# Routed rows written to fixed places per expert, four groups at a time; gathers and sums moved within covariance steps

## What is computed

```python
x = x + _L0_attn_a_ref(_layernorm(x, axis=-1), ...)      # 16 heads of 8, rotary
x = x + _L0_ffn_ref(_layernorm(x, axis=-1), ...)         # attention, then mixture of experts
x = x + _L0_attn_b_ref(_layernorm(x, axis=-1), ...)      # 16 heads of 8, covariance scores
x = x + _L0_ffn_ref(_layernorm(x, axis=-1), ...)
...
def moe_ff(x, w_gate, w1, b1, w2, b2):                   # 8 experts, 128 -> 512 -> 128
    probs = jax.nn.softmax(t @ w_gate, axis=-1)
    tw, ti = lax.top_k(probs, TOP_K)                     # TOP_K = 2
    tw = tw / jnp.sum(tw, axis=-1, keepdims=True)
    for e in range(N_EXPERTS):
        we = jnp.sum(jnp.where(ti == e, tw, 0.0), axis=-1)
        h = jax.nn.gelu(t @ w1[e] + b1[e]) @ w2[e] + b2[e]
        out = out + we[:, None] * h
```

## Time and profile before

| | us |
|---|---|
| median of 3 runs | 901.24 |
| the runs | 893.77, 901.24, 902.31 |
| the profiled execution's own time | 898.2 |
| its span, first to last instruction | 896.4 |
| busy in it: PE / DVE / ACT / POOL | 767.0 / 544.5 / 543.4 / 484.2 |
| mean granted TensorE clock | 0.923 of full speed |

### The profile page before, as it was taken

How to read it: one execution, slowest core, us unless ns; L and a number is a source line. 1 busy time by engine, 2 the same in 40 slices (tenths; PEclk the granted TensorE clock), 3 DMA queues, 4 the chain that set the end, 5 groups by cost and what they waited for, 6 DMA issues and landing times.

```text
span 896.4 us, 21301 instructions
## 1 busy us (share of the span) xinstructions
PE 767.0 (86%) x7166; PEld 546.7 (61%) x7166; DVE 544.5 (61%) x1370; ACT 543.4 (61%) x1264; POOL 484.2 (54%) x906
## 2 busy tenths in 40 slices
PE   1999999999999399697988999999999948968970
PEld 1756655666565189497964565566666525958970
DVE  4699899788988123012486887878889822211232
ACT  0377777878787256154546676787877834715640
POOL 6667678747762621504645665844777273060436
PEclk9999999999999789698999899999999977978995
DMA  9300000000000436266210000000000042635842
GB/s 274 111 3 3 3 2 3 4 3 3 4 2 4 130 107 175 79 182 175 79 38 13 16 18 5 4 3 3 3 3 3 3 124 77 173 103 143 245 124 67
DMA packets 57657, 56.29 MB, mean 63 GB/s; under 512 B 6856, under 2 KB 42448, under 8 KB 57552
## 3 DMA queue, kind: packets, MB, share of 16 engines
q1 hardware_dynamic: 39200, 39.13, 15.5%
q0 software_dynamic: 4096, 8.40, 3.2%
q10 hardware_dynamic: 14256, 7.41, 2.9%
HBM read 40.10 MB, written 14.29 MB: 61 GB/s over the span
## 4 chain that ended last, share of the span: by engine, by line
PE 56%; DVE 21%; issue 11%; POOL 7%; DMA 3%; ACT 2%; another core or an unknown queue 0%; ACTq 0%; POOLq 0%; DVEq 0%; SPq 0%
DVE M L1109 11%; PE bankO L466 11%; PE bankR L720 8%; PE bankE L707 7%; PE bankE L485 7%; PE bankE L439 6%; DVE QKV L1071 2%; POOL Yg L1578 2%; PE bankR L452 2%; PE bankE L476 2%; PE bankR L506 2%; PE bankR L536 1%; PE bankR L738 1%; PE bankR L554 1%; DMA Yg<-sorted_y,SLOT 1%
## 5 line engine op out<-in xcount | busy, mean ns | idle before, releaser
L1109 DVE TENSOR_REDUCE M<-bankR 128x2 f32<-128x512 f32 x512 | 326.4, 684 | 62.7 <-PE bankR L452 56.9
L834 ACT ACTIVATE Pr<-bankE 128x512 f32<-128x512 f32 x512 | 277.7, 595 | 129.5 <-PE bankE L439 109.1
L466 PE MATMUL bankO<-Pr,Vx 128*32 128x256 f32 x2048 | 170.5, 406 | 18.8 <-issue 16.1
L452 PE MATMUL bankR<-KQ 32*128 32x256 f32 x1024 | 171.3, 339 | 5.0 <-DVE M L1109 2.9
L439 PEld LDWEIGHTS bankE<-KQ 32*128 32x128 f32 x1024 | 79.6, 188 | 97.1 <-issue 64.2
L439 PE MATMUL bankE<-KQ 32*128 32x256 f32 x1024 | 133.3, 335 | 0.5 <-issue 0.5
L1312 DVE COPY Yb<-bankR 128x128 f32<-128x128 f32 x92 | 26.4, 290 | 167.9 <-PE bankR L720 111.1
L452 PEld LDWEIGHTS bankR<-KQ 32*128 32x128 f32 x1024 | 110.1, 191 | 17.1 <-DVE M L1109 12.8
L951 ACT ACTIVATE G<-bankE,W 128x128 f32<-128x128 f32 x368 | 101.5, 384 | 24.8 <-PE bankE L707 14.0
L707 PE MATMUL bankE<-XTT,W 128*128 128x128 f32 x736 | 105.1, 288 | 11.4 <-issue 4.6
L1578 POOL DMA_INDIRECT Yg<-sorted_y,SLOT x64 | 62.2, 971 | 95.6 <-DMA sorted_y<-Yb 42.0
(11 more groups left out here) (169 smaller groups left out, 1147.0 us busy)
## 6 DMA issues: line engine op xcount, KB each, us to landing
W<-in_w1b SPq DMA_DIRECT2D x92, 258.0 KB
sorted_y<-Yb ACTq DMA_DIRECT2D x92, 64.0 KB
XT<-sorted_u SPq DMA_DIRECT2D x20, 256.0 KB
sorted_u<-Yg SPq DMA_DIRECT2D x2, 1472.0 KB, 9.7
KQ<-MT SPq DMA_DIRECT2D x128, 4.0 KB
X<-in_x SPq DMA_DIRECT2D x8, 128.0 KB, 7.3
sorted_u<-U,SLOT POOLq DMA_INDIRECT x64
Yg<-sorted_y,SLOT POOLq DMA_INDIRECT x64
```

The source lines that it names most:

```text
L452: k = mm(dve_bank("raw", layer, b, h)[:, z * T:z * T + T], QT[rows, kb, g, z * P:z * P + P], KT[rows, kb, g, :], start=True, stop=True)
L466: k = mm(bankO[SL * j:SL * j + SL, cols], Vx[:, b % VB, kc, HG * g + j, :], Pr[:, g % 2, j, kc, :], start=(g % 2 == 0 and kc == 0), stop=( ...
L834: nc.scalar.activation(Pr[:, (h // HG) % 2, h % HG], act_bank("S", layer, b, h).rearrange("p (k q) -> p k q", k=TT), ACT.Exp, scale=EXP_SC ...
L1109: v.tensor_reduce(M[:, b % 2, :, h], dve_bank("raw", layer, b, h).rearrange("p (t k) -> p t k", t=TT), AX.X, ALU.max, negate=True).then_in ...
```

## The change

The rows of U no longer wait for the totals of a half. `sorted_u` has 1024 places (CAP) for each of the 8 experts, so a row's place needs only the counts of the groups before it. Totals and ranks are made for each block of 8 groups (`do_totals`, `do_rank`, `place_rows`), and `scatter` writes four groups at a time: at the end of steps 16 and 17, twice in step 18 (the second four after 14 of the step's scores), and four times in the mixture, the second four after tile 5 and the last after tile 14. Since a tile of an expert now begins at a row that only the totals tell, `sort_tiles` makes, beside EID, the list ROW of 23 first rows, and `load_x` reads its row from it and loads one tile at a time: 92 transfers of 64 KB, each with a register load, in place of 24. The sorted results stay compact, so a second list, SLOT_Y, is made for the gathers by `place_outputs`. The clearing grows to 8 MB, in eight transfers of 1 MB that ScalarE's queue issues at the head of steps 4 to 11, from G, which GpSimd sets to zero in step 2. `weigh` of block 1 and 3 moves ahead within its step. In the covariance steps the four gathers stand together behind `close`, ahead of `stack_k`, and `combine` goes ahead of `do_max` 4. The gathers of sequences 0 and 1 stand together as well, ahead of the normalisation of sequence 0.

```diff
+BG = GROUPS // 2
+CAP = HB * T
...
-        sorted_u = [nc.dram_tensor(f"sorted_u{k}", (NTL * P, D), F32).ap() for k in range(2)]
+        sorted_u = [nc.dram_tensor(f"sorted_u{k}", (E * CAP, D), F32).ap() for k in range(2)]
...
-            def load_x(ph, q):
-
-                half, i = divmod(GROUP[q][0], NTL)
-                n, k = GROUP[q][1], (ph * NGRP + q) % NXG
+            def load_x(ph, at):
+
+                half, i = divmod(at, NTL)
+                q, j = group_of(at)
+                k = (ph * NGRP + q) % NXG
+                r = sp.value_load(ROW[0:1, half, i:i + 1], min_val=0, max_val=E * CAP - P)
                 if i == 0:
                     sp.wait_ge(scattered[half], 16 * GROUPS * (ph + 1))
-                need(sp, x_turned, ph, q - NXG)
-                sp.dma_start(XT[:, k, 0:n, :],
-                             sorted_u[half][i * P:(i + n) * P, :].rearrange("(j p) d -> p j d", p=P)).then_inc(x_in[k], 16)
+                if j == 0:
+                    need(sp, x_turned, ph, q - NXG)
+                sp.dma_start(XT[:, k, j, :], sorted_u[half][bass.ds(r, P), :]).then_inc(x_in[k], 16)
...
-                for q in range(2 * NXG):
-                    load_x(ph, q)
+                for i in range(2 * NXG * XG):
+                    load_x(ph, i)
                 for at in range(NAT):
                     if at + NW < NAT:
                         load_w(ph, at + NW)
-                    if group_at(at - 1) is not None and group_at(at - 1) % (NGRP // 2) < NGRP // 2 - NXG:
-                        load_x(ph, group_at(at - 1) + NXG)
-                    if at == NTL - XG - 1:
-                        for q in range(NGRP // 2, NGRP // 2 + 2 * NXG):
-                            load_x(ph, q)
+                    if 2 * NXG * XG <= at + 11 < NTL:
+                        load_x(ph, at + 11)
+                    if NTL - XG <= at < NTL + XG:
+                        for i in range(2):
+                            load_x(ph, NTL + 2 * (at - NTL + XG) + i)
+                    if NTL + XG <= at < NAT - 3 * XG:
+                        load_x(ph, at + 3 * XG)
...
+            def do_rank(ph, j):
+
+
+                need(pe, placed, ph, j, 1)
+                ring_r.take(pe, ("rank", ph, j))
+                bank, n = dve_bank("rank", ph, j), BG * E
+                known = slice(0, n * (j % 2 + 1))
+                if j % 2:
+                    mm(bank[:, n:n + E], totals[:], of_expert, start=True, stop=True)
+                mm(bank[:, 0:n], below, OH[:, j * BT:j * BT + BT].rearrange("p n k e -> p (n k e)"), start=True, stop=False)
+                mm(bank[:, 0:n], totals[known, :], earlier_groups[known, of_block(j)], start=False,
+                   stop=True).then_inc(ranked.sem, 1)
+                if j % 2:
+                    ring_r.give(("rank", ph, j), sorted_, ph, j // 2, 1)
...
+            def zero(half, x):
+
+                act.wait_ge(zero_set, 1)
+                act.dma_start(sorted_u[half].rearrange("(p i) d -> p (i d)", p=P)[:, x * ZN:x * ZN + ZN],
+                              G[:].rearrange("p n c r -> p (n c r)")[:, 0:ZN]).then_inc(zeroed, 16)
+
             for ph in range(2):
                 for s in own_steps(ph):
+                    if ph == 0 and 4 <= s < 12:
+                        zero((s - 4) // 4, s % 4)
...
-                if a and LAYERS[a[0]] == "ffn" and a[1] == NB - 1:
-                    sort_rows(a[0] // 2, 0)
                 if m:
                     do_max(*m, 0)
+                if ends_block(gone2, 0):
+                    place_rows(*block_of(gone2))
...
+                if ends_block(gone, 1):
+                    weigh(*block_of(gone))
+                if a and LAYERS[a[0]] == "ffn" and a[1] == NB - 1:
+                    sort_tiles(a[0] // 2, 0)
                 if m:
                     do_max(*m, 3)
                 if rope:
                     rotate(*n, 0, 0)
+                if late(p):
+                    combine(0, p[1])
+                    norm_in(*p)
                 if m:
                     do_max(*m, 4)
                 if rope:
                     rotate(*n, 0, 1)
-                if late(p):
-                    combine(0, p[1])
-                    norm_in(*p)
                 if nxt and not late(nxt):
                     norm_in(*nxt)
...
+                if ends_block(gone, 1):
+                    copy_totals(*block_of(gone))
...
+                if ends_block(gone, 0):
                     weigh(*block_of(gone))
                 if block_of(u) is not None:
                     choose(*block_of(u))
@@ -1209,6 +1259,10 @@
                 if t:
                     residual(*t)
                     norm3_in(*t)
+                if ends_block(gone, 0):
+                    copy_totals(*block_of(gone))
+                if ends_block(gone, 1):
+                    place_rows(*block_of(gone))
...
+            def place_rows(ph, j):
+
+                half, at = j // 2, (j % 2) * BG
+                io = iota[:].unsqueeze(1).broadcast_to([P, BG, E])
+                need(dve, ranked, ph, j)
+                v.scalar_tensor_tensor(rank[:], io, float(CAP), dve_bank("rank", ph, j)[:, 0:BG * E].rearrange(
+                    "p (g e) -> p g e", e=E), ALU.mult, ALU.add).then_inc(placed.sem, 1)
+                need(dve, placed, ph, j, 2)
+                tt(rank[:], rank[:], one_hot(j * BG, BG), ALU.mult).then_inc(placed.sem, 1)
+                need(dve, placed, ph, j, 3)
+                v.tensor_reduce(place[:, at:at + BG], rank[:], AX.X, ALU.add).then_inc(placed.sem, 1)
+                need(dve, placed, ph, j, 4)
+                if ph:
+                    dve.wait_ge(scattered[half], 16 * GROUPS)
+                v.tensor_copy(SLOT_U[:, half, at:at + BG], place[:, at:at + BG]).then_inc(placed.sem, 1)
+                if j % 2:
+                    v.tensor_scalar(ntiles[:, 0], dve_bank("rank", ph, j)[:, BG * E:BG * E + E], 1.0 / P,
+                                    (P - 1) / (2.0 * P), ALU.mult, ALU.add).then_inc(sorted_.sem, 1)
+
+            def sort_tiles(ph, half):
...
+                v.tensor_reduce(row[:, 0], skip[:], AX.X, ALU.add).then_inc(sorted_.sem, 1)
                 done(11)
-                v.tensor_reduce(npast[:], past[:], AX.X, ALU.add).then_inc(sorted_.sem, 1)
+                v.scalar_tensor_tensor(row[:, 1], tile_no, float(P), row[:, 0], ALU.mult, ALU.add).then_inc(sorted_.sem, 1)
                 done(12)
-                v.tensor_scalar(EID[:, half], npast[:], float(E - 1), None, ALU.min).then_inc(sorted_.sem, 1)
+                v.tensor_scalar(ROW[:, half], row[:, 1], float(E * CAP - P), None, ALU.min).then_inc(sorted_.sem, 1)
...
+            def scatter(ph, j, part):
+
+                half = j // 2
+                need(pool, placed, ph, j)
+                need(pool, u_ready, 2 * ph + 1, 2 * j + part, 6)
                 if ph:
                     need(pool, x_turned, ph - 1, (half + 1) * NGRP // 2 - 1)
                 else:
-                    pool.wait_ge(zeroed, 2 * 16)
-                for n in range(GROUPS):
-                    b, t = divmod(half * HB * TT + n // 2, TT)
+                    pool.wait_ge(zeroed, 2 * 4 * 16)
+                for n in range(part * BG // 2, part * BG // 2 + BG // 2):
+                    b, t = divmod(j * BT + n // 2, TT)
+                    at = (j % 2) * BG + n
                     g.indirect_dma_start(sorted_u[half][:, :],
-                                         bass.IndirectOffsetOnAxis(ap=SLOT[:, half, n:n + 1], axis=0),
+                                         bass.IndirectOffsetOnAxis(ap=SLOT_U[:, half, at:at + 1], axis=0),
                                          U[:, b, t, :], None).then_inc(scattered[half], 16)
...
                 if fetched:
-                    gather(0, p[1] + 1, range(0, 1))
+                    gather(0, p[1] + 1)
                 if n:
                     if n == (3, 0):
                         clear_cov()
                     stack_k(*n)
-                if fetched:
-                    gather(0, p[1] + 1, range(1, 2))
                 if t:
                     unrope(*t)
                 if n:
                     stack_q(*n)
                     stack_v(*n)
-                if fetched:
-                    gather(0, p[1] + 1, range(2, 3))
                 if p and not early:
                     norm(*p)
-                if fetched:
-                    gather(0, p[1] + 1, range(3, 4))
...
+                        g.memset(G[:], 0.0).then_inc(zero_set, 1)
...
                         gather(0, 0)
+                        need(pool, evacuated, 0, NTL + 1)
+                        gather(0, 1)
                     step(*sequences(ph, s))
-                    if ph and s == 0:
-                        gather(0, 1)
-                    if s == STEPS - DRAIN - 1:
-                        scatter(ph, 0)
+                    if s == 16:
+                        scatter(ph, 0, 0)
+                    if s == 17:
```

(12 more changed lines are left out.)

153 lines of the change are left out of this document (86 added, 67 removed).

## The result

The changed kernel takes 906.4 us (median of 20 runs, 900.22 to 912.78), the kernel before 898.1 us (20 runs, 892.79 to 902.53): a ratio of 1.0098, 95% interval 1.0078 to 1.0119. It is 1% slower, where I forecast 873 us and a range of 847 to 904. The profiled execution has a span of 904.3 us against 896.4.

The account below looks back on a forecast made before the run. Long runs of GpSimd writes, making signals between engines up to 12 us late, were the largest loss touched; 12 + 15.6 + 5 + 2 - 8.6 - 0.6 = 25.4 us off 898.2 gave 872.8, forecast 873, range 847 to 904.

Parts of the forecast that it names:

- The two turns: From the steps to the mixture, both phases: `hidden` begins at 317.6 instead of 323.31, 6 us gained each, 12 in all.
- The part on the writes: In the turn: writes end near 300 and signals between engines are good again at 302 us instead of 314.
- What is added: Steps 16 to 18: `place_rows` 1.0 us twice, copies and totals 0.3, fours 2; 8.6 us in all; clearing G 0.6.
- The middle of the mixture: Long run of writes goes, 15.6 and 14 us; SyncE takes back 7 us a phase; 15.6 us gained.
- The 7 us for SyncE: Second half of the mixture: TensorE waits 7 us a phase for row loads that SyncE issues late.
- Writes in fours: A run of four writes delays other engines 1 us in the steps, 0 in the mixture; bounds 0 and 3 us.
- fours freeze as well: Rival: each run of four costs its 3 us in steps 16 and 17 and the mixture; 905 us, chance 0.20.
- Gathers: Gathers that now stand together in the covariance steps and the fill cost TensorE nothing by holding up signals.
- The covariance steps: Earlier sum and moved gathers: 1.2 to 1.4 us in each of 4 steps, 5 us, plus 2 in the fill.
- SyncE: SyncE's issues in turn and mixture: each row load takes 1.1 us, like a weight load, so rows come late.
- The rival by which it isn't late: Issues overlap or loads land sooner, so SyncE's waits in turns and mixture go; 848 us, chance 0.12.
- The rival of a slower SyncE: A row load needs 1.45 us, 16 us more a phase over 46 loads; 905 us, 909 at 1.5; chance 0.12.

Follow-up runs that it names:

- e1: Changed kernel without the sixteen indirect writes of the first half in steps 16 to 18 of either phase; 1.0116 of the kernel before.
- e12: Changed kernel unedited, run again on a chip of the faster sort; 1.0119 of the kernel before.
- e9: Changed kernel with the second pair's weights, totals, ranks and rows one stage later; 0.9912 of the kernel before, on a chip of the faster sort.
- e15: Same kernel as e9, run again on another chip of the faster sort; 0.9938 of the kernel before.
- e17: e9's kernel with the first eight row loads of the second half issued by GpSimd instead of SyncE; 1.0017 of the kernel before, slower sort of chip.
- e13: Kernel before with one more TensorE wait in step 17, gate product waiting for two maxima; 1.0054 of the kernel before, faster sort of chip.
- e10: e9's kernel with row loads from fixed rows (rows fetched not those of the tile's expert); 0.9685 of the kernel before.
- e6: Changed kernel with VectorE's copy of the second pair's totals ahead of two maxima in step 17; 1.0179 of the kernel before, slower sort of chip.
- e3: Changed kernel with row loads from fixed rows instead of rows read from ROW; 0.9873 of the kernel before, faster sort of chip.
- e16: Changed kernel unedited, run again on another chip of the faster sort; 1.0106 of the kernel before.
- e18: Kernel before with only the covariance part (gathers together, sum one pair of maxima sooner); 1.0045 of the kernel before, slower sort of chip.
- e2: Changed kernel with the four writes of step 17 moved to the head of step 18's writes; 1.0146 of the kernel before.

## Why the prediction was wrong, step by step

**The two turns** (12 us gained, forecast). The part on the writes held in the main: no window with GpSimd alone, and on A fours that cost nothing there (e1). On B this is not shown. There the first wait is 1.06 us, where on A it is 0.52 with the writes (e12) and without them (e1), and in e12 VectorE goes from `weigh` to the maxima without a gap. So the four writes of step 17 may have a part in what drops the clock on B. The step that failed is the one in "What is added": 1.0 us for `place_rows`, 0.3 for copies and totals. It puts the order of the work at nothing: `weigh` ahead of the maxima of step 17, and the copy of the totals ahead of the gate product. I costed the instructions and the shift of the maxima, not the order in which TensorE waits for them, and I took the clock as given. It opened waits of 1.06 and 1.79 us where the kernel before has none over 0.62, and 31 and 34 us at half clock followed. With that the scores ended 14 us later, about what the writes' end had cost, and the turns came out 3.1 us longer each. Moving the work one stage gave back 14 to 17 us on A (e9, e15); on B it was run only with e17's other edit, which has turns 4 us shorter than the changed kernel. That half clock makes the scores late is shown by the two phases of one run: 37.9 and 45.9 us with one wait (e13), 37.0 and 42.1 (e9). What exactly makes the clock fall stays open: 1.42 us came before a fall in one phase of two (e13), so did 0.89 us in e9, in both phases of e10 it did, and without the 1.79 us behind the 1.06 us the clock fell all the same (e6).

**The middle of the mixture** (15.6 us gained less 7, each phase about). The 7 us for SyncE were right: 7.6 by the trace. Over the whole kernel a row load at half the cost, 0.61 us (9.79 for sixteen) in place of 1.13, gave 21 and 18.5 us (e3, e10). What was missing: 3.1 us behind one run of four writes, and 2.4 us behind eight gathers (0.27, 1.06 and 1.05). That makes 13.1 us of the 14.5 that the first mixture falls short of the long run's 15.6. The 15.6 was itself counted short: the 21.2 us hold four half tiles, that of 359.75 among them (16 matmuls of either kind), not five, so 16.4 us were to be gained. In the second phase the waits for rows are 6.13, 1.55 and 0.40 us, 8.1 in place of 7, and 3.66 us stand behind the second four; from the 14 us this leaves 2.2 gained, and 3.2 were lost. The other 5.4 us I can't place one by one, with three stretches below full clock in it.

**Writes in fours.** "0 in the mixture, since `hidden` is three tiles ahead" failed where VectorE's `choose` and ScalarE's exponential stood behind the write: the upper bound of 3 us was the value, 3.38 for VectorE. The rival "fours freeze as well" had this mechanism and the time 905. On B VectorE or ScalarE is late beside every run of four in either mixture, and TensorE pays for one of them each time, the second, 3.09 and 3.66 us; in the A traces (e12, e16) it pays at none. That it met the time is luck, since most of its 32 us did not come about.

**Gathers** were put at nothing by the earlier trace rows, a window with four of them. Eight in a row were in the change, and TensorE's waits beside them are 2.4 us in the changed kernel and 4.5 in e18, both on B.

**The covariance steps** (7 us). 1.3 in the trace pair. Alone the part gave 8 us on A and lost 4 on B, where its steps did get 2.3 us shorter; the term was right for one sort of chip.

**SyncE.** An issue of 1.1 us held (18.16 us for sixteen); the earlier trace rows had it for weight loads only, and that a 64 KB row load costs the same came out with the change. The rival by which it isn't late is out: e3 gained 21 us by a cheaper issue. The Trainium skill (DMA: Bandwidth & Descriptors, Issuing engines are not separate DMA queues) calls a sequencer's time to initiate a transfer usually small relative to it; here the issue, with the register load in it, takes 1.13 us beside 3.0 us to landing, which isn't small. The rival of a slower SyncE (905 to 909) met the time, not the cause.

On the clock: a row first, 0.50 for 284 to 315 behind waits of 1.06 and 1.79 us. The Trainium skill (TensorE: Matmul & The Clock Gate, HAM oscillation — how this bites in real kernels) describes waits between bursts of matmuls, for transfers there, that leave the next burst cold, and says that a kernel whose work is long beside its waits stays warm. For the fall the traces bear it out in part, as above. By the second sentence the clock should have come back soon under steady work: in the first phase of e2 it did, and in e15 (0.57 for 288 to 292, 1.00 for 300 to 306), but e6 shows 30.00 us busy of 30.00 at 0.50, so there the trace differs.

## What to carry to other kernels

Before moving work onto a stage where two engines hand results to and fro, list for each moved instruction who waits behind it on its own queue and whose buffer it holds; a wait of one or two microseconds on TensorE can cost ten by the clock that follows. When a long stall is removed, ask what it was hiding: here a slow stretch, a late queue of issues, and a run of gathers all stood ready to take its place. When a variant lands on the forecast, check that it has in it what the forecast had. And measure on more than one chip before a per cent is believed.
